# Another order of TensorE's work in an attention loop, and a ring of three PSUM banks that turns round

## The reference, cut to what matters

```python
q = _lin(_lin(x, wq_w, wq_b), vq_w, vq_b)            # k and v alike
q = q.reshape(b, s, hc, H).transpose(2, 0, 1, 3)     # 32 heads, 4 batches, 1024, 16
scores = jnp.einsum('cbqh,cbkh->cbqk', q, k) / scale
attn = jax.nn.softmax(scores, axis=-1)
o = jnp.einsum('cbqk,cbkh->cbqh', attn, v)
```

## Time and profile before

| | |
|---|---|
| median of 3 runs | 2087.46 us (2086.99 to 2290.2) |
| the profiled execution | 2087.88 us, its span 2086.2 us |
| PE busy | 2033.5 us, 97% |
| DVE busy | 1644.6 us, 79% |
| ACT busy | 1318.8 us, 63% |
| granted TensorE clock | 0.986 of full speed |

### The profile page before, as it was taken

The page is one execution under the profiler, slowest core; times in us unless marked ns, Lnnn a source line. Parts: engine busy times, 40 slices in busy tenths (PEclk is TensorE's granted clock), DMA queues, the critical chain, the costliest instruction groups (busy, mean ns, idle before and its releaser), DMA issues.

```text
span 2086.2 us, 42029 instructions
## 1 busy us (share of the span) xinstructions
PE 2033.5 (97%) x12280; PEld 1160.1 (56%) x12280; DVE 1644.6 (79%) x1727; ACT 1318.8 (63%) x2429; POOL 487.9 (23%) x878
## 2 busy tenths in 40 slices
PE   9999999999999999999999999999999999999996
PEld 4788775444444444444444444444444487767774
DVE  4333356999999999999999999999999467886687
ACT  0112113888888888888888888888888743453344
POOL 0000001112212221221122122212211462464245
PEclk9999998999999999999999999999999999999997
DMA  4455835566675765776665757667757678763672
GB/s 166 138 164 150 197 109 110 85 131 134 108 136 120 120 135 99 137 139 106 129 133 106 138 118 120 131 106 137 139 103 168 225 258 322 286 228 121 230 265 96
DMA packets 214415, 315.26 MB, mean 151 GB/s; under 512 B 105424, under 2 KB 121808, under 8 KB 202064
## 3 DMA queue, kind: packets, MB, share of 16 engines
q1 hardware_dynamic: 214352, 314.47, 62.8%
HBM read 211.06 MB, written 101.19 MB: 150 GB/s over the span
## 4 chain that ended last, share of the span: by engine, by line
PE 89%; DVE 6%; ACT 1%; DMA 1%; issue 1%; POOL 1%; SPq 0%; POOLq 0%; DVEq 0%; ACTq 0%
PE psum L549 25%; PE psum L187 23%; PE psum L574 19%; PE psum L223 12%; PE psum L585 7%; PE psum L88 2%; DVE stats L1448 1%; PE psum L1368 1%; DVE y L1573 1%; ACT probs L672 1%; DVE gates L1547 1%; DVE gates L1544 1%; ACT gates L1297 1%; DMA x_block<-in_x_t_dram 0%; DVE y L1478 0%
## 5 line engine op out<-in xcount | busy, mean ns | idle before, releaser
L230 DVE TENSOR_REDUCE neg_max<-psum 128x1 f32<-128x1024 f32 x1024 | 1195.0, 1216 | 116.6 <-PE psum L223 100.0
L672 ACT ACTIVATE probs<-psum 128x512 f32<-128x512 f32 x2048 | 1069.4, 602 | 236.0 <-PE psum L549 232.7
L549 PE MATMUL psum<-q_op,k_op 50*128 50x512 f32 x2048 | 693.0, 452 | 3.8 <-ACT probs L672 3.3
L223 PE MATMUL psum<-k_op,q_op 48*128 48x512 f32 x2048 | 664.8, 491 | 0.4 <-DVE neg_max L230 0.3
L549 PEld LDWEIGHTS psum<-q_op,k_op 50*128 50x128 f32 x2048 | 337.1, 191 | 511.0 <-ACT probs L672 489.2
L574 PE MATMUL psum<-probs,v_op 128*32 128x512 f32 x3080 | 412.8, 608 | 9.3 <-issue 7.1
L223 PEld LDWEIGHTS psum<-k_op,q_op 48*128 48x128 f32 x2048 | 405.3, 315 | 13.4 <-DVE neg_max L230 5.2
L187 PE MATMUL psum<-x_wino,conv_w 128*128 128x512 f32 x1152 | 276.0, 395 | 0.2 <-DMA conv_w<-conv_w_parts_dram 0.2
L187 PEld LDWEIGHTS psum<-x_wino,conv_w 128*128 128x128 f32 x1152 | 214.5, 188 | 46.3 <-issue 0.6
L241 POOL CAST neg_max_parts<-neg_max 128x8 fp32r<-128x8 f32 x128 | 24.5, 192 | 740.2 <-DVE neg_max L230 740.2
L585 PE MATMUL psum<-probs,v_op 128*32 128x256 f32 x2032 | 163.2, 393 | 0.0
(11 more groups left out here) (105 smaller groups left out, 1707.4 us busy)
## 6 DMA issues: line engine op xcount, KB each, us to landing
q_op<-qk_parts_dram SPq DMA_DIRECT2D x384, 128.0 KB, 4.8
conv_w<-conv_w_parts_dram SPq DMA_DIRECT2D x32, 1536.0 KB, 6.7
qk_parts_dram<-qk_parts SPq DMA_DIRECT2D x128, 256.0 KB, 3.2
k_op<-qk_parts_dram SPq DMA_DIRECT2D x384, 64.0 KB, 4.9
conv_w_parts_dram<-conv_w_parts SPq DMA_DIRECT2D x16, 1536.0 KB, 7.0
attended_dram<-out SPq DMA_DIRECT2D x64, 256.0 KB, 2.8
attended_parts_dram<-o_parts SPq DMA_DIRECT2D x128, 128.0 KB, 3.6
gates<-in_ctx_dram SPq DMA_DIRECT2D x32, 512.0 KB, 7.5
```

The source lines that it names most:

```text
L223: return nc.tensor.matmul(mem["pair"][t % 2][:, lane * HALF:(lane + 1) * HALF], ops["q"][i][r, b, t:S:QT], ops["k"][i][r, b, :], start=Tru ...
L230: nc.vector.tensor_reduce(ops["max"][b][:, t:t + 1], mem["pair"][t % 2][:], AX_X, ALU.max, negate=True).then_inc(ops["maxed"], 1)
L549: nc.tensor.matmul(score_bank(k, t, last), kop[k][r, j // 2, n // 2 * P:(n // 2 + 1) * P], qop[k][r, j // 2, j % 2 * HALF:(j % 2 + 1) * HALF],
L672: nc.scalar.activation(probs[n % DEEP][:, c ^ n % 2, :], score_bank(k, t, last), ACT.Exp, scale=SCALE).then_inc(exp_done, 1)
```

## The change

`slot` is written out for a whole slot in place of a period that runs twice. Three of the eight value steps (1, 2 and 5) are computed in halves, in place of two (2 and 6); step 7 of the slot before stands behind cell 3 and unit 2, step 0 behind cell 6. Most units start with the other lane. `EVACUATE_AFTER` goes from 8 to 3. The ring of banks is turned: up to cell 7 of the iteration's 128 the bank is the cell modulo 3, from cell 8 it counts down (`turning`), so that cell 6 and cell 8 share a bank, cells 5 and 9, and, across the end of the iteration, cells 127 and 1, 126 and 2. `since` gives the distance to the last cell in the same bank, from which the wait is made; `wide_bank` is reordered to fit.

```diff
-    EVACUATE_AFTER = 8
+    TURN = 8
+    EVACUATE_AFTER = 3
...
-        wide_bank = s2_bank + [bank[0], bank[1], bank[2]]
+        wide_bank = [s2_bank[2], s2_bank[1], s2_bank[0], bank[0], bank[1], bank[2]]
...
+        def turning(cell):
+
+            return (cell if cell < TURN else 2 * TURN - 2 - cell) % RING
+
+        def since(cell):
+
+            cells = 4 * STEPS * TILES
+            return next(d for d in range(1, cells) if turning((cell - d) % cells) == turning(cell))
...
-            return s2_bank[cell % RING]
+            return s2_bank[turning(cell)]
...
-                    pe.wait_ge(exp_done, it * 4 * (STEPS * TILES) + cell + (2 if cell < 2 else 1))
+                    pe.wait_ge(exp_done, it * 4 * (STEPS * TILES) + cell + RING + 1 - since(cell))
...
-                for n in range(0, STEPS, 4):
-                    t, u = n * TILES, 2 * n
-                    shifted(it, k, t, last)
...
+                shifted(it, k, 0, last)
+                unit(it, k, 0, 1, last)
+                values_before(6)
+                shifted(it, k, 1, last)
...
```

More of the change, by code:

```diff
@@ new lines, in values_before @@
+                def values_before(n):
+                    if not (first and k == 0):
+                        values(s - 1, (k - 1) % 4, n)
+                shifted(it, k, 0, last)
+                unit(it, k, 0, 1, last)
+                values_before(6)
+                shifted(it, k, 1, last)
+                unit(it, k, 1, 0, last)
+                shifted(it, k, 2, last)
+                shifted(it, k, 3, last)
+                unit(it, k, 2, 0, last)
+                values_before(7)
+                shifted(it, k, 4, last)
@@ new lines, in slot @@
+                shifted(it, k, 5, last)
+                unit(it, k, 3, 0, last)
+                shifted(it, k, 6, last)
+                values(s, k, 0)
+                shifted(it, k, 7, last)
+                unit(it, k, 4, 0, last)
+                shifted(it, k, 8, last)
+                shifted(it, k, 9, last)
+                unit(it, k, 5, 0, last)
+                value_half(s, k, 1, 0)
+                shifted(it, k, 10, last)
+                shifted(it, k, 11, last)
+                unit(it, k, 6, 0, last)
@@ new lines, in slot @@
+                shifted(it, k, 12, last)
+                value_half(s, k, 1, 1)
+                shifted(it, k, 13, last)
+                unit(it, k, 7, 0, last)
+                shifted(it, k, 14, last)
+                value_half(s, k, 2, 0)
+                shifted(it, k, 15, last)
+                unit(it, k, 8, 0, last)
+                shifted(it, k, 16, last)
+                shifted(it, k, 17, last)
+                unit(it, k, 9, 0, last)
+                value_half(s, k, 2, 1)
+                shifted(it, k, 18, last)
@@ new lines, in slot @@
+                shifted(it, k, 19, last)
+                unit(it, k, 10, 0, last)
+                shifted(it, k, 20, last)
+                values(s, k, 3)
+                shifted(it, k, 21, last)
+                unit(it, k, 11, 0, last)
+                shifted(it, k, 22, last)
+                shifted(it, k, 23, last)
+                unit(it, k, 12, 0, last)
+                values(s, k, 4)
+                shifted(it, k, 24, last)
+                shifted(it, k, 25, last)
+                unit(it, k, 13, 0, last)
@@ L639, in _ @@
+                shifted(it, k, 26, last)
+                value_half(s, k, 5, 0)
+                shifted(it, k, 27, last)
+                unit(it, k, 14, 0, last)
+                shifted(it, k, 28, last)
+                shifted(it, k, 29, last)
+                unit(it, k, 15, 0, last)
+                value_half(s, k, 5, 1)
+                shifted(it, k, 30, last)
+                shifted(it, k, 31, last)
             for k in range(4):
```

## The result

The changed kernel took 2066.98, 2071.57, 2099.57 and 2101.03 us, median 2085.57, against a median of 2087.22 of four runs of the kernel before beside it. The ratio, 0.9917 [0.9888, 0.9945], compares the means of the runs in which the granted clock stayed high, 2069.3 us of two against 2086.7 us of three. Run again (experiment 11) it took 2073.45 (median of 12, 2065.67 to 2098.61), ratio 0.9946 [0.9916, 0.9975]. So the change gives 0.5 to 0.8%, some 11 to 17 us. I had forecast 36 us and 2051 us, with a range from 2037 to 2066: the direction is right, the size is two to three times too large, and the time lies outside the range.

What follows compares the result with a forecast made beforehand. PE's path was taken to bound the attention: 19.455 us of work plus waits 0.04, 0.215, 0.05 and 0.18 gave 19.94 a slot against 20.53. Over 61 slots, 2087.5 - 36.5 = 2051 us, range 2037 to 2066.

Steps and rivals of the forecast that it cites:

- The price list of PE: PE's times: whole value product (V) 1.00 us, half (H) 0.57, score matmuls between (block) 0.305 plus 0.12 per matmul.
- The ring: Banks at cells 1 and 8 of an iteration: turned, no wait where 0.14 us a slot was.
- rival 4: Turning the ring fails, cell 1 or 8 still waits: 0.14 us a slot given back, 2060 us; chance 0.05.
- H of step 1: First half of value step 1 on PE: waits 0.05 us for cell 7's exp, or 0.24 if released like step 0.
- Cell 29: Score cell behind the first half of step 5: waits 0.215 us a slot, once and not twice.
- Unit 9: Unit before the second half of step 2: a new wait for unit 7's reduce, 0.18 us a slot.
- the walk of DVE against PE: From step 0's start, DVE ends unit 7's reduce at 6.41 us; PE reaches unit 9 at 6.29.
- The copy: ACT's copy of sums, released by step 7: starts about 1.12 us behind it; step 0 waits 0.04 instead of 0.23.
- The ends of the attention: The last two slots, with half of the units or none, are limited by ACT's exps and give nothing.
- Rival 2: Larger waits at step 1's first half and unit 9, 0.24 us each: 20.1 to 20.2 a slot, 2061 to 2067; chance 0.13.
- Rivals 1 and 3: The first: new waits absent or cell 29's gone, 19.50 to 19.80 us a slot, 2026 to 2043; chance 0.22.
- rival 3: Slower: added half stays, starved ACT and DVE keep waits at their old sum; +18 us, 2106; chance 0.03.

Runs made afterwards that it cites:

- experiment 11: The changed kernel run once more, nothing altered: 2073.45 us, ratio 0.9946 to the kernel before.
- experiment 1: The changed kernel with the old ring (bank is the cell modulo 3): 2094.49 us, ratio 1.0042 to the kernel before.
- experiments 3 to 5: The changed kernel with one value step in one piece, each alone: step 1, 2094.85 us; step 5, 2098.28 us; step 2, 2092.19 us.
- experiment 10: Kernel before, copy behind cell 7 instead of 8: median 2109.99 us. The 2105.2 us is reported for the changed kernel with step 2 in one piece.

## Why the prediction was too far down

- **The price list of PE** (V 1.00, H 0.57, a block 0.305 and 0.12 per matmul) was right. Seven of the eleven pieces came within 0.015 of it, and with short reduces the other blocks of halves did too.
- **The ring** was right: no slot waits at cells 1 and 8, every fourth slot is as long as the others, and experiment 1 shows that without it nearly all of the gain is gone. Its rival 4 is out.
- **H of step 1** waits as a cell does (2.19 against the 2.195 that I took), not as V0 behind the copy. **Cell 29** waits 0.215, as priced (1.93). **Unit 9** waits 0.12 in place of 0.18; DVE's chain was walked rightly there.
- **The step that failed is the walk of DVE against PE, which I made for unit 9 only.** The prediction says "Unit 9 waits for the reduce of unit 7" and takes every other unit as free; units 6 and 10 were never walked. Walked in that way unit 6 comes out at a tie: by the prices its matmul is due at 936.61 + 2 x 0.12 = 936.85, and the reduce of unit 4 ends at 936.85; the release of 0.05 to 0.12 that I gave unit 9 would have been its whole wait. Unit 10 comes out free: by the forecast's own figures the reduce of unit 8 is over at V0 + 7.60, and unit 10's matmul is due at V0 + 7.73. They wait 0.175 and 0.11, since the weight load is what waits, and that is due 0.11 behind the block's start: unit 6's at 936.72, released at 936.90, unit 10's at 941.55, released at 941.66. Both units together are 0.285 a slot, 17 us, nearly the whole miss.
- **The copy.** V0 was priced at 0.04 behind its own path; it waits 0.10, since the copy starts 1.13 to 1.22 behind V7 rather than 1.12. 0.055 a slot, 3 us, as much as unit 9 gave back.
- **The ends of the attention.** I had the last two slots give nothing. From the start of the last but one to the end of the last copy they take 38.8 us where they took 37.6 (1618.56 to 1656.13 before, 1597.14 to 1635.91 after, from the timelines of PE and ACT): 1.2 us lost.
- **The rivals.** Rival 2, larger new waits (20.1 to 20.2 a slot, 2061 to 2067 us, 0.13), came nearest in size, but not by its places: H of step 1 and unit 9 were no larger than forecast. Rivals 1 and 3 are out; of rival 3, that starved engines keep waits alive, a part is true. "TensorEngine Tiling (Array Packing)", section "Key Properties" of the Trainium skill, spoke against the edit by the drain at a change of mode. The price was in my sum (0.305 per block), and experiments 3 to 5 show it hidden by waits at all three halves.

In sum: 61 slots x 0.30 (20.24 against 19.94) = 18.3 us and 1.2 of the end are missing from the forecast 36.5, which leaves 17.0, some 2071 us. The two ratios give 0.9917 x 2087 = 2070 and 0.9946 x 2087 = 2076 us, and the profile with the same start of the attention as before 2073.57. The changed kernel's executions spread over 35 us, and the longer ones have the lower mean clock (2065.67 us at 0.992, 2091.34 at 0.978, 2098.61 at 0.972); where in the program they lose it no profile of this kernel shows. The range was made of the sum's bounds alone and took in nothing of such a spread.

## What to carry to other kernels

Walk every instruction that waits against its producer, not only the one that looks tightest, and release a matmul at its weight load: here that is 0.23 us ahead of where the matmul stands in the block. A step split in two can be free if its second part fills a wait, so price a split by the pieces around it, with and without. Two changes that each give next to nothing may give the whole gain together, as the ring and the order do here: a part that makes no difference alone is not shown to be useless.

## What the runs showed that I had not expected

- A unit's wait for the reduce ends 0.05 us behind the reduce, on the weight load; the following half starts 0.79 behind that load, whether the load was held (936.90 to 937.69) or free (935.23 to 936.02). Counted from the matmul's place my prices make it 0.67, so a wait must be set against the load.
- A unit right behind a value step makes the block 0.11 us longer than a unit behind one cell (2.26 against 2.14).
- How long PE stays at 1.2 GHz when the attention begins differs between executions. The clock is back at 1.00 from 350 us in the profile after, from 370 in the one before, and from 400 in that of experiment 10, which took 2105.2 us where the fastest of that kernel took 2085.07 (windows as above):

```profile
370.00:400.00 30.00, 30.00 (x137) 11.34 (x129) 17.37 (x16) 15.20 (x30) 1.18 (x5) 0.54 0.33 50
```

- The changed kernel's times spread from 2066 to 2101 us in 16 runs. Of the kernel before, 23 of the 29 runs beside experiment 11 lie between 2081.6 and 2093.9 us, and six from 2113.8 to 2242.2 at clocks down to 0.901.
